# Moving the projection, the low parts and the value projection inside an attention batch

## The reference, cut to what matters

```python
xn = _layernorm(x, axis=-1)                       # x: 32 batches x 256 tokens x 128
ctx = xn @ We.T
influence = einsum('bqe,bke->bqk', ctx, ctx)
Q, K, V = heads(Wq), heads(Wk), heads(Wv)         # 16 heads of 8 columns
scores = einsum('bhqd,bhkd->bhqk', Q, K) * SCALE + 0.1 * influence[:, None]
attn = softmax(scores, axis=-1)
out = einsum('bhqk,bhkd->bhqd', attn, V).reshape(b, s, d) @ Wo.T
x = x + out + ffn(xn)     # ffn: 8 experts, 2 per token, 128 -> 512 -> 128
```

## Time and profile before

| | |
|---|---|
| median of 3 runs | 727.4 us (726.87 to 727.62) |
| the profiled execution | 725.8 us, its span 724.1 us |
| PE busy | 663.7 us, 92% of the span |
| DVE busy | 650.1 us, 90% |
| ACT busy | 531.9 us, 73% |
| POOL busy | 514.5 us, 71% |
| chain that ended last | PE 65%, DVE 13%, SP's queue 8%, DMA 6%, issue 5%, ACT 2% |

### The profile page before, as it was taken

The page is one execution under the profiler, slowest core; times in us unless marked ns, Lnnn a source line. Parts: engine busy times, 40 slices in busy tenths (PEclk is TensorE's granted clock), DMA queues, the critical chain, the costliest instruction groups (busy, mean ns, idle before and its releaser), DMA issues.

```text
span 724.1 us, 25378 instructions
## 1 busy us (share of the span) xinstructions
PE 663.7 (92%) x8084; PEld 448.1 (62%) x8084; DVE 650.1 (90%) x1177; ACT 531.9 (73%) x1123; POOL 514.5 (71%) x613
## 2 busy tenths in 40 slices
PE   0377899999999999799999999999999999999996
PEld 0263445555555555599999999999455555555554
DVE  8989989999999999699999999999899999898991
ACT  2593388888888888667767767777787787787885
POOL 8680477777677656077777887787688888888782
PEclk9986799999999999999999999999999999999999
DMA  8859466776676676633333333332577777877652
GB/s 249 307 170 336 135 166 169 182 200 161 175 209 173 174 191 174 160 76 96 93 96 93 97 96 90 97 92 75 142 155 179 191 178 183 173 178 187 176 122 67
DMA packets 124919, 113.37 MB, mean 157 GB/s; under 512 B 16416, under 2 KB 112416, under 8 KB 124832
## 3 DMA queue, kind: packets, MB, share of 16 engines
q1 hardware_dynamic: 115600, 90.63, 47.7%
q0 software_dynamic: 8192, 16.86, 9.6%
q10 hardware_dynamic: 1040, 4.76, 1.8%
HBM read 64.72 MB, written 47.19 MB: 155 GB/s over the span
## 4 chain that ended last, share of the span: by engine, by line
PE 65%; DVE 13%; SPq 8%; DMA 6%; issue 5%; ACT 2%; ACTq 0%; DVEq 0%
PE bank L1266 13%; PE mx L1255 13%; PE bank L1135 12%; PE bank L1113 11%; PE mx L1147 7%; DVE mx L961 6%; DMA stack<-qk_dram 6%; PE bank L1033 2%; PE bank L1247 2%; PE bank L1195 2%; DVE A L796 2%; SPq L331 2%; PE bank L1157 1%; ACT A L715 1%; PE bank L1164 1%
## 5 line engine op out<-in xcount | busy, mean ns | idle before, releaser
L715 ACT ACTIVATE A<-bank 128x512 f32<-128x512 f32 x502 | 278.2, 597 | 63.8 <-PE bank L1135 55.8
L961 DVE TENSOR_REDUCE mx<-mx 128x4 f16<-128x1024 f32 x256 | 302.7, 1205 | 19.1 <-PE mx L1147 14.7
L1135 PE MATMUL bank<-stack 113*128 113x256 f16 x1004 | 170.4, 276 | 1.3 <-ACT A L715 0.8
L761 ACT ACTIVATE rows<-mx,b 128x256 f32<-128x256 f32 x284 | 120.1, 480 | 57.7 <-PE mx L1255 55.3
L556 POOL DMA_INDIRECT slots_x<-rows,pos x128 | 123.6, 966 | 51.8 <-PE bank L1135 32.0
L570 POOL TENSOR_SCALAR rows<-rows,slot_p 128x128 f32<-128x128 f32 x142 | 124.6, 887 | 43.9 <-DVE rows L1009 43.9
L607 POOL DMA_INDIRECT rows<-slots_y,pos x128 | 121.5, 950 | 37.5 <-issue 17.3
L1113 PE MATMUL bank<-A,V 128*32 128x256 f32 x2048 | 137.9, 387 | 1.7 <-ACT A L715 1.6
L1135 PEld LDWEIGHTS bank<-stack 113*128 113x128 f16 x1004 | 72.4, 97 | 89.4 <-ACT A L715 53.8
L1266 PE MATMUL bank<-w,rows 128*128 x1704 | 107.7, 219 | 0.6 <-DVE rows L1003 0.6
L1003 DVE TENSOR_TENSOR rows<-rows 128x512 f16<-128x512 f32 x142 | 101.4, 714 | 4.9
(11 more groups left out here) (145 smaller groups left out, 684.9 us busy)
## 6 DMA issues: line engine op xcount, KB each, us to landing
stack<-ctx_rest SPq DMA_DIRECT2D x64, 256.0 KB
stack<-qk_dram SPq DMA_DIRECT2D x128, 96.0 KB
rows<-slots_x SPq DMA_DIRECT2D x71, 129.0 KB, 2.3
slots_y<-rows SPq DMA_DIRECT2D x71, 128.0 KB, 1.8
qk_dram<-hi_qk SPq DMA_DIRECT2D x64, 128.0 KB
stack<-ctx_high SPq DMA_DIRECT2D x128, 64.0 KB
slots_x<-A ACTq DMA_DIRECT2D x1, 4644.0 KB, 20.3
w_stage<-in_w SPq DMA_DIRECT2D x8, 512.0 KB
```

The source lines that it names most:

```text
L715: act.activation(A[:, n % NA, :, :].rearrange("p h s -> p (h s)"), scores(k, n)[:, :], ACT.Exp, scale=SCALE).then_inc(s_xp, 1)
L761: act.activation(h32[r % 2][:, fc, :], bank[fc][:, 0:SLOT], ACT.Gelu_apprx_tanh, bias=b1[:, bass.ds(e + fc, 1)], scale=1 / FS).then_inc(s_ ...
L961: dve.tensor_reduce(mx[:, a, 8 * qt:8 * qt + 8].rearrange("q (i e w) -> q i e w", i=2, e=2)[:, :, g % 2], MX[u % 2][:, :].rearrange("q (i ...
L1135: mm = pe.matmul(scores(k, n)[:, i * S:(i + 1) * S], stack[0:SHIFT + 1, par, h, 1, c * P:(c + 1) * P], stack[0:SHIFT + 1, par, h, 0, :], s ...
```

## The change

In TensorE's list `project` goes from the end of unit 1 to unit 2, behind `plain(2)` and `plain(3)` and in front of `shifted`. The value projection goes from between the two `shifted` of unit 3 to behind both of them in unit 4, ahead of `values`; ScalarE's copy of V goes along to unit 4. In VectorE's list the addition goes from behind R0 to behind R1, and the low parts go from behind R2 to behind R3, in front of the transposes.

```diff
 # ScalarE
-                    if u == 3 and f["m"]:
+                    if u == 4 and f["m"]:
                         act.wait_ge(s_v, b1_ + 1)
 # VectorE, behind the tensor_reduce
+                    if u == 3 and f["p"]:
+                        b3_ = s.at(3)[0]
+                        dve.wait_ge(s_hq, b3_ + 1)
+                        dve.scalar_tensor_tensor(out=lo_qk[...], in0=MISC[:, :], ...).then_inc(s_lq, 1)
+                    if f["m"]:
                         if u in (3, 7):
                             dve.wait_ge(s_red, 8 * b1_ + 4 * a + 4)
...
-                    if u == 0 and f["c"]:
+                    if u == 1 and f["c"]:
                         bc = s.at(-2)[0]
...
-                    if u == 2 and f["p"]:
-                        (the same low parts)
 # TensorE
-                        if u == 3 and f["m"]:
+                        if u == 4 and f["m"]:
                             drained(3, s, f, k)
...
+                    if u == 2 and f["p"]:
+                        drained(1, s, f, k)
+                        ...
+                        project(b3_)
                     for p in range(2):
                         if f["x"] and not (opening and u == 0):
                             shifted(p)
-                        if p == 0:
+                        if p == (1 if u == 4 else 0):
                             small_products()
...
-                    if u == 1 and f["p"]:
-                        drained(1, s, f, k)
-                        ...
-                        project(b3_)
```

More of the change, by code:

```diff
@@ L961, in attend @@
                         dve.tensor_reduce(mx[:, a, 8 * qt:8 * qt + 8].rearrange("q (i e w) -> q i e w", i=2, e=2)[:, :, g % 2], MX[u % 2][:, :].rearrange("q (i w k) -> q i w k", i=2, w=2), AX.X, ALU.max).then_inc(s_red, 1)
+                    if u == 3 and f["p"]:
+                        b3_ = s.at(3)[0]
+                        dve.wait_ge(s_hq, b3_ + 1)
+                        dve.scalar_tensor_tensor(out=lo_qk[:, :, :].rearrange("p a t -> p (a t)"), in0=MISC[:, :], scalar=1 / WS,
+                                                 in1=hi_qk[:, :, :].rearrange("p a t -> p (a t)"), op0=ALU.mult, op1=ALU.subtract).then_inc(s_lq, 1)
+                    if f["m"]:
                         if u in (3, 7):
@@ L1179, in attend @@
                             plain(v)
+                    if u == 2 and f["p"]:
+                        drained(1, s, f, k)
+                        if k == 0:
+                            pe.wait_ge(s_cntr, 2)
+                        if k == 1:
+                            pe.wait_ge(s_routed, 2)
+                        project(b3_)
                     for p in range(2):
```

## The result

The changed kernel takes 729.83 us (median of 6 runs, 729.46 to 731.1) where the kernel before takes 727.13 us beside it (median of 6, 726.2 to 728.4). The ratio is 1.004, 95% interval 1.0027 to 1.0053. So it is slower by 2.7 us, 0.4%, clear of the 0.2% that the measurement can tell. I had forecast +1.2 us and called "same" the likeliest. The time lies in the range and the direction is right; the likeliest class was the wrong one.

A forecast was written before the change was run, and what follows sets the result against it. PE was taken to set the pace, losing only 0.28 us of a step to DVE. First half +3.1, second half -1.0 and -1.8, edges +0.9 sum to +1.2 us: 728.6 us against the median of 727.4, range 725.5 to 732.

The forecast's parts named there:

- Value projection behind the pair: In unit 4, behind both `shifted` instead of splitting the pair in unit 3: -0.13 us a step, from -0.07 to -0.19.
- The projection's new place: Behind `plain(3)` in unit 2: the reordering costs PE nothing or up to 0.1 us, taken as +0.05 a step.
- The ring: Two banks: without the value projection as cover, `shifted` 9 waits for exponential 7 in unit 4; +0.27 us a step.
- Waits for R5 and R7: Second units of `plain(6)` and the next `plain(0)` no longer wait for DVE: -0.28 us a step.
- The rival in which they stay: DVE waits in unit 5 for the transposes, so the 0.28 us isn't given back: 734.5 us, chance 0.17.
- First half: Steps where ACT also scales weights: +0.45 us for a pair of steps, 7 pairs, +3.1 us.
- the cast's term: Even first-half steps: ACT's cast delays exponentials 6 and 7, `shifted` 9 is late by 0.8 us; +0.49 each, 7 steps.
- Second half: 11 steps at -0.09 us give -1.0; more cover for the stack's load before `plain(0)` gives -1.8 of possible -2.4.
- Edges: Step 16's projection is bare, 0.66 us; steps 29 and 30 get the two-bank stall: +0.9 us (0 to 1.5).
- The first rival: DVE is the bound, so steps fall: 706 us, or 717 with ACT's casts holding the first half; chance 0.14.
- The casts stay covered: First half: a late PE makes room for ACT's casts; -3.1 us, 724.3 us, chance 0.07.
- The gap only moves: DVE's idle time goes to the reciprocal, small shifts cover the two-bank stall, no load matters: 727.4 us; chance 0.12.

The follow-up runs named there:

- the ring covered again: Changed kernel with the value projection between the two `shifted` of unit 4 instead of behind both: 726.02 us, ratio 1.0018 to the kernel before.
- the kernel with the three edits: Changed kernel with value projection between unit 4's two `shifted`, even steps' cast in unit 1, step 16's projection ending unit 1: 803.02 us, ratio 1.0002.

## Why the prediction was right or wrong

What bounds the kernel: right. DVE's gap of 0.49 us is closed and the quiet step is what it was. PE got back the 0.28 us that it had waited for R5 and R7 and no more, lost as much elsewhere, and DVE's idle time came up again in front of the reciprocal, 0.60 us, as forecast. With the ring covered again a quiet step fell to 13.03 us at the same 12.41 us of DVE. The Trainium skill, Perfetto Trace Analysis, section "Identifying the Most-Contended Engine", takes the engine with the highest occupancy, and judges TensorE's headroom not by its busy matmuls but by MFU (the share of its peak rate that it reaches) and the busy share of its weight loads. DVE has 12.40 of 13.21 us in both kernels, the weight loads 7.2, and yet the chain of the quiet step has only PE on it, before and after. Here the trace goes against that rule.

The terms, forecast against the profiled execution after. Its own total is +5.1 us (730.92 against 725.8), while the medians differ by 2.7.

- Value projection behind the pair, forecast -0.13: the chain has 0.54 + 0.42 for it, so -0.17. The projection's new place, forecast +0.05, is +0.05 (0.81 + 0.44 for 0.66 + 0.54).
- The ring, +0.27: it is +0.27, but half of it stands where I had none, at the pair of unit 3 (0.16), since exponential 5 is late too.
- Waits for R5 and R7, -0.28: right. The rival in which they stay is out.
- The sum for a quiet step, -0.09: it is 0.00 against 13.21. Some 0.1 us goes at the start of the step, where PE now comes earlier than ACT's exponentials and its copy of oT (a pair of 0.59 us).
- First half, +3.1: +4.37. **This is the step that failed in size**: the cast's term, +0.49 for an even step. It is worth 0.72 (0.74 in the changed kernel, less the 0.02 of the kernel before). I let exponential 4 start 0.60 us behind `shifted` 4, and it starts 0.78 behind it (195.50 and 194.72), since the high parts themselves start 0.28 behind; exponential 6 starts 2.68 us behind and not 2.52. And I left out that `shifted` 7 waits as well. The mechanism is shown: cutting the cast takes 0.74 us off, moving it takes 0.73. An odd step, forecast +0.05 (-0.09 and 0.14), is 0.02 shorter.
- Second half, -1.0 for the steps and -1.8 for the load: the steps gave -0.1 and the load the whole -2.4. In the waits from us 545 to 703 of the kernel after, the load is nearly gone:

```profile
PE mx L1148 <- DMA stack<-qk_dram: 0.2, 1, 0.2
```

  But that the change bought this is not shown. The kernel before with the cast cut has the order of the kernel before in the second half, and in its trace these eleven steps take 145.43 us, hardly more than the 145.16 of the changed kernel:

```profile
535.60:681.03 145.43, 144.81 (x1652) 79.15 (x1651) 136.44 (x222) 115.73 (x232) 119.42 (x119) 1.00 0.77 181
```

  So nearly all of the 2.4 us can be the one execution of the kernel before that I read. I took a wait of a single trace for a property of the kernel.
- Edges, +0.9: they are +3.3. Step 16 alone has +2.5 (13.86 for 11.39), of which 0.6 to 0.9 is the order and 1.6 the clock. Step 17 is 0.45 shorter, and steps 29 and 30 have +0.27 each (12.68 for 12.41). The stretch behind the last step takes 19.88 us for 19.20, at a granted clock of 0.86 for 0.96. I had said that the clock is no term. For the steps that holds; for the opening and the end it doesn't, some 2.2 us of this execution's 5.1.

Against the profiled execution the sum is 3.9 us too small: 1.3 for the first half, 0.2 for the second, 2.4 for the edges. Against the medians it is 1.5 us too small, as much as the whole width of "same", and so "same" was not what came. That the medians lie so much nearer is in part luck: the clock in step 16 and the wait for the load differ between traces of kernels that have the same order there. The first rival (DVE the bound) was given 0.14 and has nothing for it. "The casts stay covered" was given 0.07 and was refuted by the two kernels with the cast cut. "The gap only moves" was right on the gap and wrong on the ring, whose stall was not covered.

## What to carry to other kernels

Idle time on a busy engine is worth what the chain pays for it. Before closing a gap, look which pieces of the pacing engine are longer than their work; here they were 0.28 us of a step and not 0.49. When a piece leaves its place, price what it covered. With a ring of two banks, whatever stands between the pieces that fill it gives the engine that empties it time to do so. The longest instruction on that engine (here a cast of 0.95 us) decides how much is laid bare, and it belongs where its engine waits anyway. A wait that one trace shows may be gone in the next execution: look at a second one before counting it as a gain.

## What the runs showed of the hardware

TensorE's granted clock can fall without a long pause. In step 16 of the changed kernel PE waited 0.92 us and 0.65 us for R0 and R1 and was busy for 1.93 of these 3.50 us. It then ran at a mean of 0.56 of full speed for 3.70 us, the 1.2 GHz level for most of it; the six matmuls of the projection took 1.46 us in place of 0.83. With the cast early, a kernel with the same opening, the waits were 0.93 and 0.64 us and PE again busy for 1.93 us of 3.50, and the clock stayed at 1.00 and the step at 12.30 us.

Chips differ more than the kernels: 802.84 us against 726.21 us for the same kernel before. The loss lies in the attention steps (about 15 us for 13.2) and not in the expert tiles, where the stretch between the two halves took 225.97 us on the slow chip and 225.84 on the first. Step 16 stands out: it takes 26 to 28 us in all four traces of the slow chip, with pauses of PE of 5.83 and 3.90 us in the kernel with the three edits and a mean clock of 0.70. In most other steps the work and the granted clock are what they were, and the pauses aren't at one instruction. Slower transfers don't show either: the packets of queue q1, which moves most of the bytes, took 42.9% of 799.3 us there and 47.7% of 724.1 us on the first chip, about the same time. I have no cause.
